# A four-layer graph network: scatters that wait pair by pair, a lighter merge, and table_t work moved to later stages

## What is computed

```
x = x + L0_gnn(layernorm(x), edges, weights)   # row norm, then twice: elu(A @ (x W) + b); A[dst, src] = sum of edge weights
x = x + L0_ffn(layernorm(x))                   # 8 experts, top 2
x = x + L1_gnn(layernorm(x), edges)            # GRU-made weights; twice: normalised counts of edges, dst <- src
x = x + L1_ffn(layernorm(x))                   # 32 experts, top 1
x = x + L2_gnn(layernorm(x), edges)            # counts of edges, dst <- src
x = x + L2_ffn(layernorm(x))                   # pooled routing, 8 experts, top 2, layernorm
x = x + L3_gnn(layernorm(x), edges, weights)   # B[src, dst]: the weights, taken the other way round
x = x + L3_ffn(layernorm(x))                   # 16 experts, top 2, layernorm
```

## Time and profile before

| | us |
|---|---|
| median of three runs | 3033.27 |
| the profiled execution | 3032.36 |
| its span | 3030.6 |
| PE busy | 2428.5 (80%) |
| DVE busy | 1485.6 (49%) |
| ACT busy | 1097.6 (36%) |
| POOL busy | 1745.6 (58%) |
| scatters into table_pairs, 392 | 625.8 |
| scatters into table_t, 392 | 618.1 |

### The profile page before, as it was taken

How to read it: one execution, slowest core, us unless ns; L and a number is a source line. 1 busy time by engine, 2 the same in 40 slices (tenths; PEclk the granted TensorE clock), 3 DMA queues, 4 the chain that set the end, 5 groups by cost and what they waited for, 6 DMA issues and landing times. The chain is left out here.

```text
span 3030.6 us, 39957 instructions
## 1 busy us (share of the span) xinstructions
PE 2428.5 (80%) x12303; PEld 1595.6 (53%) x12304; DVE 1485.6 (49%) x4880; ACT 1097.6 (36%) x2433; POOL 1745.6 (58%) x1310
## 2 busy tenths in 40 slices
PE   3344438999999986857979959599897999949994
PEld 1122213444446445746858846486565454649993
DVE  8899985654433246346664363634234000163335
ACT  7799972232211014444333324333334000023333
POOL 4888878888887854767848724484600300034543
PEclk9999999999999997988989979799998999979997
DMA  9999869987869954345535433554302544166674
GB/s 332 291 287 293 284 205 282 278 257 224 222 129 294 286 134 142 103 152 126 124 86 121 92 95 105 151 123 99 85 0 92 148 123 136 54 227 197 209 210 141
DMA packets 391813, 525.72 MB, mean 173 GB/s; under 512 B 161964, under 2 KB 302554, under 8 KB 381645
## 3 DMA queue, kind: packets, MB, share of 16 engines
q1 hardware_dynamic: 238142, 460.63, 44.6%
q0 software_dynamic: 127728, 41.96, 13.4%
q10 hardware_dynamic: 25760, 20.90, 2.1%
HBM read 346.64 MB, written 176.71 MB: 173 GB/s over the span
## 5 line engine op out<-in xcount | busy, mean ns | idle before, releaser
L659 POOL DMA_INDIRECT table_pairs<-sums,index_to x392 | 625.8, 1596 | 160.2 <-issue 117.9
L659 POOL DMA_INDIRECT table_t<-sums,index_from x392 | 618.1, 1577 | 122.4 <-issue 118.6
L1709 PE MATMUL sum_psum<-wide,parts 128*128 128x512 f32 x1800 | 431.5, 394 | 6.4 <-DVE parts L1745 3.0
L1709 PEld LDWEIGHTS sum_psum<-wide,parts 128*128 128x128 f32 x1800 | 340.8, 190 | 80.3 <-DVE parts L1745 3.9
L1265 PE MATMUL sum_psum<-abuf,y 128*128 128x512 f32 (+1 forms) x700 | 308.5, 576 | 22.6 <-DMA abuf<-table_pairs 20.4
L1265 PE MATMUL sum_psum<-abuf,acc 128*128 128x512 f32 (+1 forms) x700 | 296.5, 564 | 0.4 <-ACT partial L1218 0.3
L978 PE MATMUL sum_psum<-abuf,y 128*128 128x512 f32 (+1 forms) x700 | 272.5, 549 | 17.9 <-ACT y L869 17.9
L535 PE MATMUL merge_psum<-part,acc 128*128 128x6 bf16 x980 | 71.0, 167 | 239.3 <-DVE pass_on L609 135.0
L1571 ACT ACTIVATE wide<-abuf 128x512 fp32r<-128x512 f16 (+1 forms) x264 | 148.6, 573 | 247.8 <-PE sum_psum L1709 233.9
L535 PEld LDWEIGHTS merge_psum<-part,acc 128*128 128x128 bf16 x980 | 56.8, 104 | 322.5 <-issue 320.1
L1265 PEld LDWEIGHTS sum_psum<-abuf,y 128*128 128x128 f32 x700 | 126.4, 193 | 170.6 <-issue 147.1
(11 more groups left out here) (508 smaller groups left out, 4269.5 us busy)
## 6 DMA issues: line engine op xcount, KB each, us to landing
abuf<-table_pairs SPq DMA_DIRECT2D x240, 512.0 KB, 5.5
table_pairs<-zero SPq DMA_DIRECT2D x50, 1600.0 KB, 5.8
abuf<-table_counts SPq DMA_DIRECT2D x90, 640.0 KB, 4.4
table_t<-zero SPq DMA_DIRECT2D x25, 1600.0 KB, 5.5
abuf<-table_t SPq DMA_DIRECT2D x150, 256.0 KB, 2.7
m_x_wa<-in_L_ffn_w_dram SPq DMA_DIRECT2D x64, 512.0 KB, 4.0
table_counts<-peeled ACTq DMA_DIRECT2D x150, 128.0 KB
tokens<-y SPq DMA_DIRECT2D x15, 640.0 KB, 3.3
```

What stands on the lines that cost most here:

```text
L659: nc.gpsimd.indirect_dma_start(table[:, :], bass.IndirectOffsetOnAxis(ap=index[:, g, j:j + 1], axis=0), k.sums[:, g, j, 0:width], None, co ...
L1709: mm = nc.tensor.matmul(k.sum_psum[:, b % 2, f, 0:n], parts[:, v, c, f * P:(f + 1) * P], k.wide[:, j % WIDENED, 0:n], start=(c == 0 and v ...
```

## The change

Constants: `BUILT` 27 to 22, `NORM_AT` 12 to 8, `RARE_AT` gone.

*Scatters.* POOL waits before each pair of scatters for the pair two back (same parity), instead of before each half line for the same half one line back.

*Merge.* Only the upper two columns of a unit are compared with the next unit, and only with its lower two (256 wide), all by ACT: two Abs and two Relu. DVE's fifth compare is gone. The passed sums stay fp32 in one write; PE's products with them fall from 16 to 4. Indices are placed line by line for the first four lines, then four lines at a time (`placed_by` counts). The row norm's sums come from ACT, one instruction a unit, and DVE does the roots at one point.

*table_t.* In prep only 8 of its 25 clears remain; 17 go to SP's queue in the m0 experts stage, from a stretch of `k.y` that DVE zeroes. Its lines: l0 19 to 0, l1a 9 to 11, l1b 9 to 11, m1 route 0 to 3, m1 pairs 0 to 2, l2 9 to 11, the pooled stage 3 to 2 + 9. In l0 the rare gathers follow the last line of `table_pairs`.

```diff
 def spread_edges(...):
-    each = UNIT * 16
+    each = HALF * 16
-            if beside is not None:
-                for b in RARE_AT.get(g - first, ()):
-                    beside(pool, b)
-            for half in range(2):
-                if g > begin:
-                    pool.wait_ge(laid[half], (g - begin) * each)
-                for j in range(half * UNIT, (half + 1) * UNIT):
+            for part in range(BLANKS // HALF):
+                before = (g - begin) * BLANKS // UNIT + part // 2
+                if before:
+                    pool.wait_ge(laid[part % 2], before * each)
+                for j in range(part * HALF, (part + 1) * HALF):
                     nc.gpsimd.indirect_dma_start(
                         table[:, :], bass.IndirectOffsetOnAxis(ap=index[:, g, j:j + 1], axis=0),
-                        k.sums[:, g, j, 0:width], None, compute_op=ALU.add).then_inc(laid[half], 16)
+                        k.sums[:, g, j, 0:width], None, compute_op=ALU.add).then_inc(laid[part % 2], 16)
...
 def merge_edges(...):   # PE, add_up
             for i in range(UNIT):
+                receives = u > 0 and i < HALF
...
-                for j in range(UNIT if u else 0):
+                for j in range(HALF if receives else 0):
                     mm = nc.tensor.matmul(to, k.later[:, (u - 1) % 3, j, i * P:(i + 1) * P],
...
-            for j in range(BY_ACT):    # ACT, compare
+            for j in range(HALF):
...
-            if u + 1 < UNITS:          # DVE, compare
-                nc.vector.scalar_tensor_tensor(
-                    k.later[:, u % 3, BY_ACT, :], own_rows(u + 1), column(k.edge_key, u, BY_ACT),
-                    k.mask[:, 0:UNIT * P], ALU.is_equal, ALU.mult,
-                    accum_out=column(k.more, u, BY_ACT)).then_inc(matched, 1)
...
-                nc.vector.scalar_tensor_tensor(k.rest[:], first.unsqueeze(2).to_broadcast([P, UNIT, 2]), 1.0, total,
-                                               ALU.is_equal, ALU.mult).then_inc(split, 1)
...
+                nc.vector.scalar_tensor_tensor(k.pass_on[:, u % 2, :, :, 0],
+                                               k.rank[:, g, upper].unsqueeze(2).to_broadcast([P, HALF, 2]), 1.0,
+                                               k.sums[:, g, upper, :], ALU.is_equal, ALU.mult).then_inc(passed, 1)
...
+def lines_together(g):
+    if g < ALONE:
+        return range(g, g + 1)
+    first = ALONE + (g - ALONE) // TOGETHER * TOGETHER
+    return range(first, min(first + TOGETHER, LINES))
+
+def placed_by(g):
+    return 2 * len({lines_together(n) for n in range(g + 1)})
...
-                        pool.wait_ge(k.merged, 2 * (g + 1))
+                        pool.wait_ge(k.merged, placed_by(g))
...
+def unit_rows_act(nc, k, act, step):
+    if 0 <= step < TILES:
+        nc.scalar.activation(k.y[:, step, :], k.x[:, step, :], ACT.Copy, accum_out=one(k.ln_work[:, 4, :], step))\
+            .then_inc(k.unit_counted, 1)
...
-                clear_back(nc, k, block, back)
+                clear_back(nc, k, block, back, k.zero[:], 0, BACK_SOON)
...
+        def clear_rest(block):
+            zero = k.y[:, :, :].rearrange("p t f -> p (t f)")[:, TILES * D - NP:TILES * D]
+            blank = k.sem("zero_blank")
+
+            @block.vector
+            def _(dve):
+                nc.vector.memset(zero, 0.0).then_inc(blank, 1)
+            clear_back(nc, k, block, back, zero, BACK_SOON, TILES, blank)
...
-                some(19)(block, lambda pool, b: rare_gather(nc, k, pool, peel, b))
+                @block.gpsimd
+                def _(pool):
+                    for b in range(BLOCKS):
+                        rare_gather(nc, k, pool, peel, b)
```

More of the change, by code:

```diff
@@ L341, in _, with clear_back @@
                 done += 1
-def clear_back(nc, k, block, table):
+def clear_back(nc, k, block, table, zero, first, last, blank=None):
     cleared = k.sem("back_clear")
@@ L349, in _ @@
     def _(sp):
[L350 to L353, removed]
+        if blank is not None:
+            sp.wait_ge(blank, 1)
+        for t in range(first, last):
+            if t > first:
+                sp.wait_ge(cleared, 16 * (t - first))
+            sp.dma_start(table[t * P * NP:(t + 1) * P * NP, :].rearrange("(p n) a -> p (n a)", p=P), zero)\
                 .then_inc(cleared, 16)
-        sp.wait_ge(cleared, 16 * TILES)
+        sp.wait_ge(cleared, 16 * (last - first))
 def load_x(nc, k, block, x):
@@ L604, in settle @@
[L604 to L616, removed]
+                dve.wait_ge(matched, UNIT * (u + 1))
@@ new lines, in settle, with place @@
+                nc.vector.scalar_tensor_tensor(k.pass_on[:, u % 2, :, :, 0],
+                                               k.rank[:, g, upper].unsqueeze(2).to_broadcast([P, HALF, 2]), 1.0,
+                                               k.sums[:, g, upper, :], ALU.is_equal, ALU.mult).then_inc(passed, 1)
+        def place(lines):
+            own, many = slice(lines.start, lines.stop), len(lines)
+            score = k.score[:, 0:many, :]
+            turn = placed_by(lines.start) - 2
+            dve.wait_ge(matched, UNIT * 2 * lines.stop)
+            dve.wait_ge(ahead, HALF * min(2 * lines.stop, UNITS - 1))
+            nc.vector.scalar_tensor_tensor(score, k.more[:, own, :], 2.0, k.rank[:, own, :], ALU.mult, ALU.add)\
@@ L629, in _, with spread_edges @@
                 settle(u - 1)
-            if u >= 2 and u % 2 == 0:
-                place(u // 2 - 1)
+            if u >= 2 and u % 2 == 0 and lines_together(u // 2 - 1).stop == u // 2:
+                place(lines_together(u // 2 - 1))
         settle(UNITS - 1)
-        place(LINES - 1)
+        place(lines_together(LINES - 1))
     k.taken = taken
-def spread_edges(nc, k, block, laid, table, index, width, first, lines, begin=0, ready=None, last=False,
-                 beside=None):
-    each = UNIT * 16
+def spread_edges(nc, k, block, laid, table, index, width, first, lines, begin=0, ready=None, last=False):
+    each = HALF * 16
     @block.gpsimd
@@ L1149, in _ @@
                 if b < BLOCKS - 1:
[L1150 removed]
+                    needed = sp.value_load(k.bound[0:1, b:b + 1], min_val=LANDS, max_val=LANDS * LINES)
                 for half in range(2):
[L1152 removed]
+                    sp.wait_ge(landed[half], needed if b < BLOCKS - 1 else LANDS * LINES)
             if i >= ring:
@@ L2089, in _ @@
                     pool.wait_ge(held.blank, TILES + 1)
+            if meanwhile is not None:
+                meanwhile(block)
             if add is not None:
@@ L2971, in _ @@
                                 normalize(tile)
+            sooner(block)
             @block.gpsimd
@@ L3344, in layer @@
                     dense_layer(nc, k, block, name, table, weight, finish, loads=loads, **more)
-                    if more.get("peel"):
-                        meanwhile(block, lambda pool, b: rare_gather(nc, k, pool, peel, b))
-                    else:
-                        meanwhile(block)
+                    meanwhile(block)
         def routed(m, func, router, by_expert, bias, mode, w1, b1, w2, b2, relu_out, into, weighted=False,
-                   residual=False, beta=None, last=None):
+                   residual=False, beta=None, last=None, meanwhile=None):
             with ExitStack() as scope:
```

167 lines of the change are left out of this document (95 added, 72 removed).

## The result

The changed kernel takes 3195.46 us (median of four runs, 3190.09 to 3199.77) against 3035.23 before (four runs, 3029.77 to 3041.07): a ratio of 1.0527, 95% interval 1.05 to 1.0553. The forecast was 3150, between 3095 and 3200, and slower with a chance of 0.95. The sign held. The time lies inside this range, 4.5 us from its upper end, and 10 us outside the narrower one of the forecast's own sum, 3115 to 3185; the loss is 160 us where 117 were forecast. Its profiled execution took 3194.76 us, its span is 3193.0.

The account below looks back on a forecast made before the run. Bound stage by stage by the last engine: POOL's scatter count in prep, PE's sixth block in l0, DVE later. 3032.4 + 34 (prep and l0) + 3 (clears) + 80 (moved lines) = 3150 us, range 3095 to 3200, own range 3115 to 3185.

Parts of the forecast that it names:

- The merge: In prep, 2.4 us a unit, ending near 290 instead of 450; worth nothing by itself.
- the 3.5 us from which the merge would bind: In prep, POOL's scatters set the pace unless a merge unit takes over 3.5 us.
- Prep's end: l0's first scatter at 374.2 without stalls, 388.7 with 14.5 us of stalls, 62 sooner than before.
- a little under a quarter of the full price: Prep's stalls from the new pair wait: 14.5 us of a full 64 for landings of 7.0.
- The row that the prediction leaned towards: Profile row of scatter landings, taken as over all scatters: 2.9 least, 3.2 median, 9.3 most.
- l0: Sixth block on PE at 856 against 821.8, +34: 27 lines of 15.75 us, stalls, 10 for last landing and load.
- its second term that was too small: Stalls of the new pair wait in l0: landings of 6.15, 1.2 us a line over 27 lines, 32 us.
- The moved lines: Scatters end five later stages late: l1a +6, l1b +16, route +22.5, pairs +13, l2 +17; pooled 0; +80 with stalls.
- The clears in m0: 17 clears moved into m0's experts share the rings with gathers: +3 us, between 0 and +20.
- The landings hold nothing: Rival, 20%: landings stay under 5.55 us, so no pair waits; l0 some 2 us sooner, 3108 in all.
- Landings of 7.0 throughout l0: Rival, 13%: pair waits in l0 cost 2.9 us a line, 78 us instead of 32; 3196 in all.
- the sign that the prediction gave for it: POOL's waits on its own table_pairs scatters in prep and l0: over 90 us would show the 7.0 rival.

Follow-up runs that it names:

- e2: Kernel before with only the table_t lines moved as in the change, its half-line wait kept: 3117.66 us, ratio 1.0285.
- e3: Changed kernel with the table_t lines where they were (l0 19, l1a 9, l1b 9, l2 9, pooled 3): 3101.01 us, ratio 1.0231.
- e6: Changed kernel with BUILT at 27 again instead of 22: 3188.35 us, ratio 1.0499.
- e4: Changed kernel with all 25 clears of table_t in prep again: 3194.6 us (two runs).
- e1: Kernel before with only the wait of each pair of scatters for the pair two back: 3110.23 us, ratio 1.0257.
- e5: Kernel before with each pair of scatters waiting for the pair three back, on four counts: 3035.8 us, ratio 1.0007.

## Why the prediction held, and where its terms were off

*The merge.* Right in its worth, wrong in its size. DVE's reduce answers to the earlier trace rows:

```profile
L606 DVE TENSOR_REDUCE sums<-merge_psum x98: 173/183/184, 36.9 to 313.6; 128x8 f32<-128x24 f32 x98
```

2.85 us a unit instead of 2.4, because PE took DVE's place as the bound: "PE's sum becomes shorter" was wrong. The merge's groups on PE:

```profile
L555 PE MATMUL merge_psum<-pass_on,acc 128*128 128x6 f32 x776 | 187.4, 359 | 0.0
L551 PE MATMUL merge_psum<-part,acc 128*128 128x6 bf16 x980 | 67.3, 167 | 10.8 <-DVE pass_on L612 7.8 <-DVE acc L597 0.8 <-issue 0.2
```

The passed sums in fp32 need 776 matmuls of 359 ns, 187.4 us together, where before 1552 in bf16 took 70.5 us. It stayed under the 3.5 us from which the merge would bind, so nothing hung on it.

*Prep's end.* l0's first scatter was forecast for 388.7 and came at 410.45. The failed step is the stall in prep: "a little under a quarter of the full price" of a landing of 7.0, 14.5 us. The waits cost 31 us there, about half of the full price of 64; the rest of the 38 is scatters 0.01 us longer, waits for the merge and one gap of 4.1 us that the trace puts down to nothing. The row that the prediction leaned towards could not tell it. Its landings "over all scatters" are those of 96 table_t scatters in later stages, and none is of table_pairs; in the DMA view of the kernel before, only the second of these rows has a time to landing:

```profile
table_pairs<-sums,index_to POOLq DMA_INDIRECT x392
table_t<-sums,index_from POOLq DMA_INDIRECT x392, 3.2
```

Its 9.3 is a single scatter of the pooled stage. What the waits of the changed kernel met can be estimated from the stalls: the longest, 4.7 us idle behind a slack of 5.55, makes a landing of about 10. The DMA share of prep was at hand, and says that prep is a full stretch nearly throughout, up to its last clear. The window of the kernel before, its last two numbers the DMA share (0.91) and GB/s:

```profile
40.00:430.00 390.00, 157.65 (x2576) 76.62 (x2576) 361.80 (x1701) 350.30 (x862) 321.51 (x209) 1.00 0.91 290
```

*l0.* The 27 lines took what was forecast within 2 us, and that is in part luck. The waits cost 45 us where the prediction put 32, its second term that was too small. The lines without them took 11 us less than 27 x 15.75, because a scatter held POOL for 1.603 us on the mean in l0, where it was 1.660 before. l0 began 21.7 us later than forecast (410.45 for 388.7), its lines took 1.7 longer, and one thing lay on top: the sixth block waited not for the last line (867.9 + 1.9 + 10 = 880) but for the fifth block, which waits for line 44 and keeps PE for 80.9 us: 887.6, 8 us more. The prediction named one chain where two end close together. Together 856 + 21.7 + 1.7 + 8 = 887.4.

*The moved lines.* Right, stage by stage, and e2 and e3 show them without the wait. The one that was off is m1 pairs, +22.0 for +13. Of the 9 us, POOL's timeline shows 2.0 in the first scatter, which waits 2.31 us for results to land, 1 in a stall, 1 in longer scatters; its drain is 1.5 longer than taken. Its gathers end 3.7 us later within the stage. In e2 and e6 this stage lost 16.7 and 17.4, so some 5 us of the 22 don't come from the lines; e4 has them too. They go with the granted clock: in the first 30 us of the stage it was 0.69 on the mean in the change and in e4, with 124 and 125 matmuls done, and 0.83 to 0.86 in the kernel before, e2 and e6, with 149 to 155. The change, then e2 (the third number from the end is the clock):

```profile
1927.00:1957.00 30.00, 25.84 (x124) 17.15 (x125) 5.02 (x11) 9.98 (x27) 20.64 (x22) 0.69 0.50 136
...
1856.50:1886.50 30.00, 25.97 (x155) 17.87 (x156) 6.47 (x14) 12.19 (x33) 22.30 (x24) 0.86 0.56 148
```

In the change the clock rose to 1.00 (2.4 GHz) 18.5 us into the stage, in e2 8.4 us into it, after PE had been nearly idle at the end of the route stage in both (3.04 us busy of the 40 before). Why it rose later is not shown.

The borders of the other stages, where POOL's last scatter and its first work in the next stage stand together (l1b to route, route to pairs, l2 to pooled):

```profile
1841.99 1.55 POOL L663 DMA_INDIRECT table_t<-sums,index_from  x1 [0.30 <-issue]
1851.02 0.41 POOL L2118 MEMSET m_hidden<- 1x384 f32 x1 [7.48 <-POOLq L3210]
...
1921.53 1.55 POOL L663 DMA_INDIRECT table_t<-sums,index_from  x1 [0.31 <-issue]
1927.73 1.02 POOL L2634 DMA_INDIRECT m_y_xin<-tokens,gather_i  x1 [4.65 <-POOLq L2078]
...
2260.27 1.54 POOL L663 DMA_INDIRECT table_t<-sums,index_from  x1 [0.30 <-issue]
2269.84 1.54 POOL L663 DMA_INDIRECT table_t<-sums,index_from  x1 [8.03 <-POOLq L3210]
```

Where before POOL idled 19.88 us at the first of these and 28.35 at the second, it is now the last to arrive, and the others wait; DVE at the first:

```profile
1851.10 0.08 DVE L685 MEMSET ln_work<- 128x25 f32 x1 [19.20 <-PEq L3210]
```

*The clears in m0.* +3.9 for +3, and e4 gives 5.3 back: right within 3 us.

*The rivals.* "The landings hold nothing" is out. The fixed 2.0 us that the Trainium skill gives for a small DMA (DMA: Bandwidth & Descriptors, "Anatomy of one DMA — SWDGE (gpsimd) path") fits no stretch here: of the landings that the trace has, all of table_t scatters, the least is 2.9 and the greatest 8.3. The section "Latency and other measured facts" of the same page of the Trainium skill, by which access to HBM grows under load, is what the trace agrees with: POOL stalls behind a 5.55 us slack in the stretches with the DMA engines 0.95 to 1.03 busy and in none of those at 0.22 to 0.25.

The time lies at "Landings of 7.0 throughout l0" (3196), and that is chance. This rival puts 78 us of stalls into l0, where 45 were measured, and it leaves prep as forecast, where the larger miss lies. The 95.2 us of POOL's waits meet the sign that the prediction gave for it (over 90), but they count the 0.30 before each scatter; without these they are 76, against the 47 that were forecast.

## What to carry to other kernels

A wait on an earlier DMA costs nothing as long as its slack, counted in starts of the same queue, is longer than the slowest landing, and when it is shorter, each landing that outlasts it delays the whole chain behind it. Take the landing from the stretch in which the wait stands and not the median over the run, and see that the row is of these scatters at all. Before an engine is made faster, see whether what it feeds is bound by count and pace elsewhere; here a merge 1.4 us a unit quicker brought 9 us at most, together with BUILT and the clears, since POOL's scatters set the pace. Work moved onto a queue is free only while its last piece, and its landing, come before the stage's other engines are done; read that from the queue's idle time at the stage's end, not from its busy share.

## What the runs showed of the hardware unasked

In the profile of the changed kernel the granted clock fell to 0.51 in the 14 us from 20 on, in which PE was busy for 1.51 us, and stayed at 0.50 (1.2 GHz) through the merge. In e3, with the same instructions up to there and 1.49 us of 14, it stayed at 1.00 (2.4 GHz). The windows of the change, then those of e3:

```profile
20.00:34.00 14.00, 1.51 (x5) 0.59 (x5) 11.16 (x37) 2.20 (x2) 0.00 (x0) 0.51 1.01 428
...
130.00:230.00 100.00, 94.06 (x679) 71.58 (x676) 82.40 (x377) 72.08 (x263) 76.33 (x50) 0.50 0.88 287
```

```profile
20.00:34.00 14.00, 1.49 (x5) 0.59 (x5) 11.16 (x37) 2.19 (x2) 0.00 (x0) 1.00 1.01 428
...
130.00:230.00 100.00, 94.05 (x680) 71.59 (x677) 82.38 (x377) 72.06 (x263) 75.29 (x49) 1.00 0.90 293
```

PE is as busy, with as many matmuls, at either level, and the merge's last reduce starts at 313.6 in the change and at 313.5 in e3. The narrow matmuls are not the whole reason, since those of 512 columns in it (L530) took 587 ns on the mean at either level. Nor is the execution slower: its time of 3194.76 us, at a mean clock of 0.852, lies among the other three (3190.09 to 3199.77, at 0.913 to 0.917). Matmuls' ends are modelled in the profile, so whether the record of the clock is at fault the runs don't say.

The scatters into table_pairs took 1.543 us (median) in the kernel before, e1, e3 and e5, and 1.554 to 1.556 in the change, e2, e4 and e6, the kernels that have no table_t lines in l0. It makes 4 us over 392; why, stays open.
